# Moving the end of one attention and its router to another PSUM bank, with new orders for the queues

## The chip, the cores and the metric

The kernel runs on one core of one Trainium2 chip. The metric is the device time of one execution in microseconds. Before the change three runs gave 3598.25, 3603.09 and 3603.4 us, a median of 3603.09 us.

## The reference, cut to what matters

The input is 16 sequences of 512 rows with 128 channels. Two layers follow each other, and in each an attention and a feed-forward part work side by side on the same normalised input. In the first layer the feed-forward part is itself an attention (with its own layer norm, a convolution and rotary positions) followed by a mixture of experts.

```python
x = L0_attn_x                                   # 16 x 512 x 128
xn = layernorm(x)
x = x + L0_attn(xn, W_K, W_Q, W_V, W_O) \       # 16 heads of 64
      + L0_ffn(xn, ...)                         # _attn (16 heads of 8), then _moe
xn = layernorm(x)
x = x + L1_attn(xn, ...) + L1_ffn(xn, ...)      # flash blocks of 64; fp4 rounding

def _L0_ffn_ref(x, ...):
    x = x + _attn(x, ...)       # softmax(q k / sqrt(8)) v, then @ proj_w
    x = x + _moe(x, ...)        # layernorm, logits = h @ router_w, argmax of 4 experts
```

The change concerns the end of `_attn` (division by the softmax sum, the product with `proj_w`, the residual) and the start of `_moe` (layer norm, logits, argmax, and the rank of each row among the rows of its expert).

## The kernel before

The 16 sequences go through a software pipeline. `run(i, nxt, nn, prv)` is written for each engine and issues, interleaved, the work of four sequences: the wide attention and the experts of sequence `i` (called dense), the end of the narrow attention of `i` (after), the narrow attention of the next one (ahead), the first norm and projections of the one after that (early), and the second layer of the one before (behind). A loop turn of this kind is called a sequence here. Each engine works its own queue in order. The order is written out by hand in `ORDERS` (line 140), one list of named steps for each engine, and `walk` calls them. Semaphores, named after what is done, join the engines. SyncE has an order of its own: `keep_xn`, `project_v` (which loads `xres`), `load_sorted`, `load_x`, `shift_rows`, `split` 0 and 1 (nine loads each of the stacks `qst` and `kst`), `store_out`.

PSUM is one tensor `ps` of 8 banks of 512 columns. Banks 0 to 3 are a ring for the wide attention (`kq`, `scores`) and serve the experts later. Bank 4 takes `v`, `z`, `transpose1`, `project`, `attend`. Banks 5 and 6 take the narrow attention: `project_v` (5), `row_max` (5 and 6 in turn), `exps` (the same), and before them the end of the narrow attention of the sequence before: `divide` (5 and 6 in turn), `join` (5), `project_y` (6), `transpose3` (5), `route` (6), `rank` (5). Bank 7 takes the second layer, from `transpose2` to `down1`.

The steps that the text below speaks of:

- `divide(t)`: TensorE turns `ys` (line 1753), VectorE takes the reciprocal of the sums and multiplies (lines 1293, 1294). `join`: TensorE turns the result (through the helper at line 1538), ScalarE copies it (960). `project_y`: product (1763), VectorE adds the residual (1301). `begin`, `ln3_stats`, `ln3_root`, `ln3_apply`: VectorE. `transpose3`, `route` (1773): TensorE; VectorE's `route` finds the expert. `rank` (1781 to 1786); `place` on VectorE ends with the semaphore `placed` (1359), for which `scatter` on GpSimd and `project_v` on TensorE wait.
- `scores(p, t)`: TensorE (1584, 1587), then the row maximum on VectorE (1210), then the exponential on ScalarE (877). Each waits for the unit two before it in the ring. `norm(p)`: VectorE (1181) and GpSimd (722) make `vn`, on which `z(p)` (1601) waits. `kq` (1561) is copied by ScalarE (858).
- `transpose2` (1538), `keys1` (1796), `queries1` (1804), `values1` (1810), `scores1` (1819): start of the second layer of the sequence before; each is copied from bank 7 by ScalarE or VectorE before the next one may write it.
- `row_max(u)`: TensorE (1703, 1705), VectorE (1275), 44 units. `exps(u)` (1722, 1724): 44 units, ScalarE (945). `attend` (1743).
- `round_h(t, k)`: the fp4 rounding, k = 0 to 2 on VectorE, the last on GpSimd (lines 798 to 800). `transpose_hq(t)` (1877) waits for it, `down1` (1884) for all four, and VectorE adds the result (1464).
- `gather` on GpSimd (789, 792) waits until the expert results are stored; `take_over` on VectorE (1367) waits for what it fetches.

Of the kernel before, what the change touches and what calls it, by code (L numbers as in the profile page):

```python
# [7 lines left out]
ALU = mybir.AluOpType  # L8
ACT = mybir.ActivationFunctionType
# [8 lines left out]
NT = T // P  # L18
# [117 lines left out]
for _p in range(PAIRS):  # L136
# [25 lines left out]
        ("row_max", 39), ("scores", 7, 1), ("row_max", 40), ("row_max", 41), ("probs_T1", 1, 3), ("scores", 7,
        2), ("row_max", 42), ("z", 6), ("scores", 7, 3), ("row_max", 43), ("mix1", 1), ("project1",),
        ("shift_rows",), ("z", 7), ("sort",), ("exps", 0), ("exps", 1), ("ao",), ("gate", 0), ("exps", 2),
        ("value", 0), ("gate", 1), ("exps", 3), ("exps", 4), ("transpose1",), ("value", 1), ("turn", 0),
        ("attend", 0, 0), ("exps", 5), ("exps", 6), ("transpose_xq",), ("down", 0), ("gate", 2), ("value", 2),
        ("exps", 7), ("exps", 8), ("turn", 1), ("exps", 9), ("attend", 0, 1), ("exps", 10), ("attend", 0, 2),
        ("exps", 11), ("attend", 0, 3), ("gate1", 0), ("down", 1), ("exps", 12), ("exps", 13), ("up1", 0),
# [113 lines left out]
def build_layers(nc, w, x, consts, out, h_sorted, y_sorted):  # L282
    B = x.shape[0]
    with ExitStack() as ctx:
# [540 lines left out]
        def _(act):  # L825
# [21 lines left out]
            def run(i, nxt, nn, prv):  # L847
# [1079 lines left out]
```

## Time and profile before

| | |
|---|---|
| median of three runs | 3603.09 us |
| the profiled execution | 3598.52 us |
| its span, first to last instruction | 3596.7 us |
| mean granted TensorE clock | 0.937 |
| TensorE matmul busy | 3086.5 us, 86% |
| VectorE busy | 2093.3 us, 58% |
| ScalarE busy | 1787.1 us, 50% |
| GpSimd busy | 860.3 us, 24% |

Read it from the busiest engine: what counts is where TensorE stands idle and for whom it waits there. The list of waits gives the sum of each kind, the timeline the place. As the pipeline repeats, one sequence in the middle stands for the others, and the windows say whether it does. The granted clock is 1.00 at 2.4 GHz and 0.50 at 1.2 GHz.

### The profile page before, as it was taken

The page shows a single profiled execution, that of the slowest core. Times are in us where ns is not written, and L with a number is a line of the kernel's source. Part 1 is how long each engine was busy: PE and PEld are TensorE (multiplying, and loading weights), DVE is VectorE, ACT ScalarE, POOL GpSimd, SP SyncE. Part 2 cuts the span into 40 slices and gives each one's busy share as a digit, 9 for nine tenths or more (in the row PEclk, how much of TensorE's full clock was granted, in tenths as well). Part 3 has the DMA queues.
Part 4 walks back from the last instruction along what each step waited for, and adds up shares of the span by engine and source line. Part 5 has one row for each costly group of instructions (what it writes and reads, how often), then busy time and mean ns, then how long its engine had stood idle before and what let it go on. Part 6 is the DMA issues. An engine that isn't in the chain of part 4 may idle for free.

```text
span 3596.7 us, 53224 instructions
## 1 busy us (share of the span) xinstructions
PE 3086.5 (86%) x19535; PEld 1705.8 (47%) x19535; DVE 2093.3 (58%) x4810; ACT 1787.1 (50%) x4252; POOL 860.3 (24%) x1140
## 2 busy tenths in 40 slices
PE   2689898998989899998989889898988989898864
PEld 1245455454545545454545545454554545454432
DVE  5454665756566575657656565665656566554432
ACT  0245555555545455555545555554555555455421
POOL 0000222313222131323123132312213131222323
PEclk7699999999999999999999999999999999999965
DMA  4130303020020302002030301103020110200000
GB/s 104 20 44 1 52 2 47 9 36 20 13 43 2 55 2 44 12 17 40 1 55 2 44 12 22 35 2 55 2 44 12 24 31 7 47 2 14 6 11 3
DMA packets 112901, 89.39 MB, mean 25 GB/s; under 512 B 11203, under 2 KB 107269, under 8 KB 112645
## 3 DMA queue, kind: packets, MB, share of 16 engines
q1 hardware_dynamic: 93956, 70.25, 12.8%
q0 software_dynamic: 4096, 8.40, 0.8%
q10 hardware_dynamic: 14592, 7.34, 0.7%
q8 instruction: 159, 2.61, 0.3%
q14 instruction: 98, 0.79, 0.1%
HBM read 27.05 MB, written 16.19 MB: 12 GB/s over the span
## 4 chain that ended last, share of the span: by engine, by line
PE 59%; DVE 12%; POOL 10%; issue 9%; ACT 5%; DMA 2%; SPq 1%; POOLq 0%; ACTq 0%; DVEq 0%
PE ps L1584 6%; PE ps L1601 6%; PE ps L1819 4%; PE ps L1743 4%; PE ps L1722 4%; PE ps L1656 3%; PE ps L1645 3%; PE ps L1623 3%; DVE nma L1210 3%; PE ps L1632 3%; PE ps L1574 2%; PE ps L1703 2%; PE ps L1884 2%; PE ps L1561 2%; PE ps L1587 2%
## 5 line engine op out<-in xcount | busy, mean ns | idle before, releaser
L877 ACT ACTIVATE share_a<-ps,nma 128x128 f32<-128x128 f32 (+3 forms) x1024 | 530.9, 525 | 443.7 <-DVE nma L1210 442.5
L1210 DVE TENSOR_REDUCE nma<-ps 128x2 f32<-128x256 f32 (+3 forms) x512 | 420.1, 823 | 407.5 <-PE ps L1587 405.4
L945 ACT ACTIVATE share_z<-ps 128x512 f32<-128x512 f32 (+1 forms) x704 | 378.3, 559 | 372.1 <-PE ps L1724 241.7
L1275 DVE TENSOR_REDUCE nmx<-ps 128x1 f32<-128x384 f32 (+3 forms) x704 | 426.1, 635 | 173.9 <-PE ps L1705 162.4
L722 POOL TENSOR_TENSOR vn<-va,rla 128x512 f32<-128x512 f32 x128 | 133.4, 1042 | 1359.1 <-DVE rla L1181 1359.1
L1601 PE MATMUL ps<-share_a,vn 128*64 128x512 f32 (+3 forms) x2048 | 351.4, 492 | 35.7 <-POOL vn L722 34.7
L1703 PE MATMUL ps<-kst,qst 96*128 96x128 bf16 (+3 forms) x1024 | 269.6, 317 | 71.1 <-DMA kst<-part 34.4
L1722 PE MATMUL ps<-qst,kst 99*128 99x512 bf16 (+3 forms) x1024 | 261.6, 304 | 28.2 <-ACT share_z L945 14.9
L798 POOL TENSOR_TENSOR share_s<-share_s 128x352 f32<-128x352 f32 (+1 forms) x80 | 80.1, 1001 | 770.7 <-DVE share_s L1084 770.5
L1601 PEld LDWEIGHTS ps<-share_a,vn 128*64 128x64 f32 x2048 | 150.8, 151 | 227.9 <-issue 154.2
L1584 PE MATMUL ps<-kq_odd 64*128 64x128 f32 (+3 forms) x1024 | 220.5, 508 | 38.7 <-ACT share_a L877 36.9
L1561 PE MATMUL ps<-xnTd,wkqT 128*128 128x512 f32 x512 | 245.3, 601 | 1.6
L1584 PE MATMUL ps<-share_g 64*128 64x128 f32 (+3 forms) x1024 | 209.9, 486 | 39.5 <-ACT share_a L877 37.6
L1743 PE MATMUL ps<-share_z,vones 128*32 128x512 f32 (+3 forms) x2048 | 193.8, 451 | 15.2 <-ACT xnTd L921 12.3
L1705 PE MATMUL ps<-up_b,ident_b 128*128 128x128 bf16 x1024 | 205.6, 228 | 0.0
L877 ACT ACTIVATION_READ_ACCUMULATOR share_a<-ps,nma 128x1 f32 x1024 | 203.1, 198 | 0.0
L1722 PEld LDWEIGHTS ps<-qst,kst 99*128 99x128 bf16 x1024 | 99.4, 98 | 216.3 <-ACT share_z L945 110.9
L1724 PE MATMUL ps<-low_b,ident_b 128*128 128x128 bf16 x1024 | 195.9, 221 | 0.0
L1703 PEld LDWEIGHTS ps<-kst,qst 96*128 96x128 bf16 x1024 | 103.1, 101 | 174.7 <-DVE nmx L1275 102.7
L1819 PE MATMUL ps<-share_q,share_s 128*128 128x512 f32 x256 | 151.1, 673 | 32.4 <-ACT share_s L982 24.7
L1574 PE MATMUL ps<-wvT,xnTd 128*128 128x128 f32 x1024 | 147.4, 288 | 29.2 <-ACT share_z L882 28.8
L1587 PEld LDWEIGHTS ps<-up_b,ident_b 128*128 128x128 bf16 x1024 | 58.4, 97 | 236.8 <-issue 221.4
(250 smaller groups left out, 5727.0 us busy)
## 6 DMA issues: line engine op xcount, KB each, us to landing
qst<-part SPq DMA_DIRECT2D x144, 128.0 KB
kst<-part SPq DMA_DIRECT2D x144, 128.0 KB
share_r<-h_sorted SPq DMA_DIRECT2D x16, 448.0 KB, 3.5
y_sorted<-share_a ACTq DMA_DIRECT2D x16, 448.0 KB, 3.0
xin<-in_L_attn_x SPq DMA_DIRECT2D x16, 256.0 KB, 3.9
xk<-xn SPq DMA_DIRECT2D x16, 256.0 KB, 17.5
xres<-in_L_attn_x SPq DMA_DIRECT2D x16, 256.0 KB
out<-xn SPq DMA_DIRECT2D x16, 256.0 KB, 17.4
```

What stands on the lines that cost most here:

```text
L877: activation(pa[:, h % 4, OFF[t]:OFF[t] + P * (t + 1)], ps[:, b + k, 0:P * (t + 1)], ACT.Exp, bias=nma[:, h, t:t + 1], accum_out=la[:, h, ...
L945: activation(pt[:, n % 2, h % 4:h % 4 + k, 0:wd], src, ACT.Exp, scale=SCALE_B)\
L1210: v.tensor_reduce(nma[:, 2 * p:2 * p + 2, t], ps[:, b:b + 2, 0:P * (t + 1)], AX.X, ALU.max, negate=True).then_inc(amax, 1)
L1275: v.tensor_reduce(nmx[:, h:h + k, t], src, AX.X, ALU.max, negate=True).then_inc(bmax_ready, 1)
L1561: ins = mm(ps[:, b + z, :], wkqT[:, z, 2 * DA * p:2 * DA * (p + 1)], xnTd[:, :], start=True, stop=True)
L1574: ins = mm(ps[:, 4, tile(t)], xnTd[:, tile(t)], wvT[:, 2 * DA * p:2 * DA * (p + 1)], start=True, stop=True)
L1584: mm(ps[:, b + k, 0:P * (t + 1)], kq[p % 2][rows, 0, tile(t)], kq[p % 2][rows, 1, 0:P * (t + 1)], start=True, stop=False)
L1601: ins = mm(ps[DA * k:DA * k + DA, 4, 0:P * (t + 1)], vn[:, h % 4, t, :], pa[:, h % 4, OFF[t]:OFF[t] + P * (t + 1)], start=(t == NT - 1), s ...
L1703: mm(ps[:, b, o:o + wd], qst[0:SHIFT_ROW, h, tile(t)], kst[0:SHIFT_ROW, h, 0:wd], start=True, stop=False)
L1722: mm(ps[:, b, o:o + wd], kst[0:SHIFT_ROW + PARTS, h, tile(j)], qst[0:SHIFT_ROW + PARTS, h, j * P:T], start=True, stop=False)
L1743: ins = mm(ps[32 * k:32 * k + 32, 4, j * P:T], vones[:, c0:c0 + 32], pt[:, n % 2, k, 0:T - j * P], start=(j == 0), stop=(j == NT - 1))
L1819: mm(ps[:, 7, :], qbd[:, 2 * p:2 * p + 2, :].rearrange("c h q -> c (h q)"), k1T, start=True, stop=False)
```

## The change

The six steps of the end of the narrow attention go from banks 5 and 6 to bank 7. For this TensorE's `divide` 1 to 3 wait until VectorE has read the one before, and `divide` 0 waits for the last add of the second layer; `project_v` no longer waits for `placed`, and `transpose2` does. All five lists in `ORDERS` are new. What the text below speaks of: on TensorE the divides are spread further apart, `project_y` comes ahead of `kq` 2 and next to it, `project_v` comes right after `z` 0, `rank` after `scores` 2,0, `up1` 3 ahead of `attend` 2,3, `transpose_hq` 2 after `turn_x`, `transpose_hq` 3 after `exps` 40, and `down1` ahead of `attend` 3,2. On VectorE `take_over` comes after `scores` 0,2, `ln2_stats` after `ln3_apply`, `split` 1 after `project` 1,1. On GpSimd `scatter` comes after `norm` 2, and `gather` after the last `round_h`.

```diff
 pool=[
-        ("norm", 0), ("norm", 1), ("spread_queries1",), ("scatter",), ("norm", 2), ("shift1", 0), ("shift1",
+        ("norm", 0), ("norm", 1), ("spread_queries1",), ("norm", 2), ("scatter",), ("shift1", 0), ("shift1",
...
-        ("gather",), ("round_h", 3, 3),
+        ("round_h", 3, 3), ("gather",),
...
 pe, the first half:
-        ("kq", 0), ("divide", 0), ("v", 0), ("divide", 1), ("kq", 1), ("scores", 0, 0), ("divide", 2),
-        ("divide", 3), ("v", 1), ("scores", 0, 1), ("join",), ("scores", 0, 2), ("project_y",), ("scores", 0,
-        3), ("kq", 2), ("scores", 1, 0), ("scores", 1, 1), ("scores", 1, 2), ("z", 0), ("v", 2), ("scores", 1,
-        3), ("transpose3",), ("kq", 3), ("route",), ("scores", 2, 0), ("scores", 2, 1), ("scores", 2, 2),
-        ("z", 1), ("rank",), ("v", 3), ("scores", 2, 3), ("kq", 4), ("transpose2",), ("project_v",),
-        ("keys1",), ("scores", 3, 0), ("queries1",), ("row_max", 0), ("values1",), ("row_max", 1), ("row_max",
+        ("kq", 0), ("divide", 0), ("v", 0), ("divide", 1), ("kq", 1), ("divide", 2), ("scores", 0, 0), ("v",
+        1), ("scores", 0, 1), ("divide", 3), ("scores", 0, 2), ("join",), ("scores", 0, 3), ("project_y",),
+        ("kq", 2), ("scores", 1, 0), ("scores", 1, 1), ("scores", 1, 2), ("z", 0), ("project_v",),
+        ("transpose3",), ("v", 2), ("scores", 1, 3), ("route",), ("kq", 3), ("scores", 2, 0), ("rank",),
+        ("scores", 2, 1), ("scores", 2, 2), ("z", 1), ("v", 3), ("scores", 2, 3), ("kq", 4), ("transpose2",),
+        ("keys1",), ("row_max", 0), ("row_max", 1), ("queries1",), ("values1",), ("scores", 3, 0), ("row_max",
...
 pe, the end:
-        33), ("attend", 2, 3), ("down", 6), ("exps", 34), ("up1", 3), ("exps", 35), ("exps", 36), ("exps",
-        37), ("exps", 38), ("turn_x",), ("attend", 3, 0), ("exps", 39), ("exps", 40), ("exps", 41), ("attend",
-        3, 1), ("exps", 42), ("exps", 43), ("transpose_hq", 2), ("attend", 3, 2), ("transpose_hq", 3),
-        ("attend", 3, 3), ("down1",),
+        ("down", 5), ("turn", 6), ("up1", 3), ("attend", 2, 3), ("exps", 34), ("down", 6), ("exps", 35),
+        ("exps", 36), ("exps", 37), ("exps", 38), ("turn_x",), ("transpose_hq", 2), ("attend", 3, 0), ("exps",
+        39), ("exps", 40), ("transpose_hq", 3), ("exps", 41), ("attend", 3, 1), ("exps", 42), ("exps", 43),
+        ("down1",), ("attend", 3, 2), ("attend", 3, 3),
...
@@ project_v (TensorE)
                         pe.wait_ge(xnTd_ready, count(i, DENSE["xnTd_ready"], 1))
-                        pe.wait_ge(placed, count(i, AHEAD["placed"], 1))
@@ divide (TensorE)
                     if t == 0:
                         pe.wait_ge(by_ready, count(i, AHEAD["by_ready"], 4))
-                    if t >= 2:
-                        pe.wait_ge(yn_ready, count(i, AHEAD["yn_ready"], t - 1))
+                        if prv is not None and (type(prv[0]) is not int or prv[0] + prv[1]):
+                            pe.wait_ge(out_ready, count(prv, BEHIND["out_ready"], 0))
+                    else:
+                        pe.wait_ge(yn_ready, count(i, AHEAD["yn_ready"], t))
                     for g in range(4):
-                        ins = tr(ps[:, 5 + t % 2, tile(g)], ys[:, g, tile(t)], idn)
+                        ins = tr(ps[:, 7, tile(g)], ys[:, g, tile(t)], idn)
@@ transpose2 (TensorE)
                     pe.wait_ge(xn2_ready, count(prv, BEHIND["xn2_ready"], 4))
+                    if i is not None:
+                        pe.wait_ge(placed, count(i, AHEAD["placed"], 1))
                     transpose_tiles(xn2, 7).then_inc(xn2T_psum, 1)
```

## Rows read from the trace of the kernel before

**Rows 1.** The page: the span, and busy time of the engines.
```profile
span 3596.7 us, 53224 instructions
PE 3086.5 (86%) x19535; PEld 1705.8 (47%) x19535; DVE 2093.3 (58%) x4810; ACT 1787.1 (50%) x4252; POOL 860.3 (24%) x1140
```
**Rows 2.** Windows between two `down1` adds: us, busy by engine, PEclk, DMA share, GB/s.
```profile
1199.22:1407.33 208.11, 188.75 (x1219) 105.53 (x1218) 129.00 (x298) 111.03 (x265) 53.77 (x71) 0.97 0.15 25
...
1615.45:1820.55 205.10, 183.51 (x1219) 103.64 (x1218) 129.14 (x299) 111.13 (x265) 53.81 (x71) 0.99 0.16 25
...
2445.31:2653.35 208.04, 187.11 (x1219) 104.82 (x1218) 128.99 (x298) 111.24 (x265) 53.78 (x71) 0.98 0.16 25
```
**Rows 3.** List of waits, whole span: us in total, times, longest us.
```profile
PE ps L1877 <- POOL share_q L800: 50.5, 18, 9.2
```
**Rows 4.** Timeline of TensorE, end of a sequence: start us, us, instruction [idle before].
```profile
1186.20 1.06 PE L1743 MATMUL ps<-share_z,vones 128*32 128x512 f32 x8 [0.77 <-ACT xnTd L921]
...
1193.66 0.55 PE L1877 MATMUL ps<-ident,share_q 128*128 128x128 f32 x3 [2.37 <-POOL share_q L800]
...
1194.78 4.33 PE L1884 MATMUL ps<-wdT,share_s 128*128 128x128 f32 x24
```
**Rows 5.** Timeline of GpSimd in the same stretch.
```profile
1185.43 0.37 POOL L789 TENSOR_TENSOR turn_g<-vones 1x1 f32<-1x1 f32 x1 [4.22 <-DMA y_sorted<-share_a]
1185.96 1.06 POOL L792 DMA_INDIRECT yg<-y_sorted,place_i  x1 [0.15 <-issue]
...
1189.83 0.94 POOL L792 DMA_INDIRECT yg<-y_sorted,place_i  x1 [0.30 <-issue]
1190.80 0.95 POOL L798 TENSOR_TENSOR share_s<-share_s 128x352 f32<-128x352 f32 x1
```
**Rows 6.** Timeline of VectorE in the same stretch, the last operation of `round_h` 3,2.
```profile
1186.17 0.34 DVE L1084 TENSOR_SCALAR share_s<-share_s 128x352 f32<-128x352 f32 x1
```
**Rows 7.** Timeline of TensorE, the first 42 us of the next sequence.
```profile
1200.67 0.60 PE L1753 MATMUL ps<-ident,share_r 128*128 128x128 f32 x4
...
1205.36 1.15 PE L1753 MATMUL ps<-ident,share_r 128*128 128x128 f32 x8 [0.40 <-DVE share_r L1294]
...
1214.91 0.49 PE L1584 MATMUL ps<-kq_odd 64*128 64x128 f32 x4 [0.86 <-ACT share_a L877]
...
1221.78 1.16 PE L1574 MATMUL ps<-wvT,xnTd 128*128 128x128 f32 x8 [0.69 <-ACT share_z L882]
...
1230.36 0.92 PE L1584 MATMUL ps<-share_g 64*128 64x384 f32 x4 [1.52 <-ACT share_a L877]
...
1231.43 4.06 PE L1601 MATMUL ps<-share_a,vn 128*64 128x512 f32 x16
...
1236.18 1.16 PE L1574 MATMUL ps<-wvT,xnTd 128*128 128x128 f32 x8 [0.40 <-ACT share_z L882]
...
1240.96 0.66 PE L1538 MATMUL ps<-ident,xn 128*128 128x128 f32 x4 [0.57 <-DVE xn L1064]
```
**Rows 8.** Timeline of VectorE, `divide` 0 of that sequence.
```profile
1204.72 0.26 DVE L1293 RECIPROCAL rb<-ps 128x16 f32<-128x16 f32 x1
1205.01 0.29 DVE L1294 TENSOR_TENSOR share_r<-ps,rb 128x128 f32<-128x128 f32 x1
```
**Rows 9.** Timeline of TensorE, `z` 1 two sequences later.
```profile
1647.67 2.37 PE L1601 MATMUL ps<-share_a,vn 128*64 128x512 f32 x16
```
**Rows 10.** Timeline of ScalarE, the copy of `transpose2`.
```profile
1241.65 0.59 ACT L970 COPY share_s<-ps 128x512 f32<-128x512 f32 x1 [0.29 <-PE ps L1538]
```
**Rows 11.** Timeline of SyncE's queue: the issue of the `kst` loads.
```profile
1200.27 13.93 SPq L671 DMA_DIRECT2D kst<-part  x9
```
**Rows 12.** Window in which the loads end (columns as in rows 2).
```profile
1230.00:1235.00 5.00, 4.64 (x20) 1.89 (x22) 2.79 (x14) 2.46 (x10) 1.04 (x1) 0.69 0.23 72
1235.00:1240.00 5.00, 4.60 (x32) 2.47 (x28) 3.08 (x12) 1.26 (x3) 0.00 (x0) 0.97 0.00 0
```
**Rows 13.** Timeline of TensorE, last but one sequence, `transpose_hq` 3.
```profile
3455.89 0.90 PE L1877 MATMUL ps<-ident,share_q 128*128 128x128 f32 x3 [9.23 <-POOL share_q L800]
```

More of the change, by code:

```diff
@@ L162 @@
[L162 to L166, printed above, removed]
@@ new lines @@
+        41), ("row_max", 42), ("z", 6), ("scores", 7, 3), ("row_max", 43), ("mix1", 1), ("project1",),
+        ("shift_rows",), ("z", 7), ("sort",), ("exps", 0), ("exps", 1), ("ao",), ("gate", 0), ("value", 0),
+        ("exps", 2), ("exps", 3), ("transpose1",), ("transpose_xq",), ("gate", 1), ("value", 1), ("turn", 0),
+        ("exps", 4), ("attend", 0, 0), ("exps", 5), ("exps", 6), ("gate1", 0), ("down", 0), ("gate", 2),
+        ("exps", 7), ("exps", 8), ("value", 2), ("turn", 1), ("exps", 9), ("attend", 0, 1), ("exps", 10),
@@ new lines @@
+        ("attend", 0, 2), ("exps", 11), ("attend", 0, 3), ("exps", 12), ("up1", 0), ("down", 1), ("exps", 13),
+        ("project", 0, 0), ("gate", 3), ("exps", 14), ("exps", 15), ("project", 0, 1), ("value", 3), ("turn",
+        2), ("gate1", 1), ("exps", 16), ("attend", 1, 0), ("exps", 17), ("exps", 18), ("down", 2), ("exps",
+        19), ("attend", 1, 1), ("exps", 20), ("exps", 21), ("gate", 4), ("attend", 1, 2), ("exps", 22),
+        ("exps", 23), ("attend", 1, 3), ("value", 4), ("turn", 3), ("exps", 24), ("up1", 1), ("project", 1,
@@ new lines @@
+        0), ("down", 3), ("gate", 5), ("transpose_hq", 0), ("value", 5), ("turn", 4), ("exps", 25),
+        ("project", 1, 1), ("exps", 26), ("gate1", 2), ("down", 4), ("attend", 2, 0), ("exps", 27), ("exps",
+        28), ("up1", 2), ("gate", 6), ("exps", 29), ("exps", 30), ("value", 6), ("transpose_hq", 1), ("turn",
+        5), ("exps", 31), ("attend", 2, 1), ("exps", 32), ("attend", 2, 2), ("exps", 33), ("gate1", 3),
+        ("down", 5), ("turn", 6), ("up1", 3), ("attend", 2, 3), ("exps", 34), ("down", 6), ("exps", 35),
@@ L190 @@
[L190 to L193 removed]
+        ("divide", 0), ("divide", 1), ("divide", 2), ("scores", 0, 0), ("scores", 0, 1), ("divide", 3),
@@ new lines @@
+        ("scores", 0, 2), ("take_over",), ("scores", 0, 3), ("project_y",), ("begin",), ("ln3_stats",),
+        ("scores", 1, 0), ("scores", 1, 1), ("norm", 0), ("ln3_root",), ("scores", 1, 2), ("ln3_apply",),
+        ("ln2_stats",), ("scores", 1, 3), ("route",), ("scores", 2, 0), ("scores", 2, 1), ("norm", 1),
+        ("scores", 2, 2), ("place",), ("ln2_root",), ("scores", 2, 3), ("ln2_apply",), ("row_max", 0),
+        ("row_max", 1), ("values1",), ("row_max", 2), ("row_max", 3), ("row_max", 4), ("row_max", 5),
@@ L207 @@
[L207 to L208 removed]
+        43), ("mix1", 1), ("norm", 7), ("project1",), ("shift_rows",), ("ln0_stats",), ("ln0_root",),
+        ("round_x", 0), ("round_x", 1), ("round_x", 2), ("ln0_apply",), ("ln1_apply",), ("add_ao",), ("gate",
+        0), ("value", 0), ("gate", 1), ("value", 1), ("gate", 2), ("conv",), ("up1", 0), ("project", 0, 0),
@@ L232 @@
-        ("exps", 32), ("down", 5), ("turn", 6), ("gate1", 3), ("exps", 33), ("attend", 2, 3), ("down", 6),
-        ("store_y",), ("exps", 34), ("exps", 35), ("exps", 36), ("exps", 37), ("exps", 38), ("turn_x",),
-        ("exps", 39), ("exps", 40), ("exps", 41), ("exps", 42), ("exps", 43), ("transpose_hq", 2),
-        ("transpose_hq", 3), ("attend", 3, 3),
[4 rows of a table added]
+        ("kq", 5), ("scores", 4, 0), ("scores", 4, 1), ("scores", 4, 2), ("z", 3), ("v", 5), ("scores", 4, 3),
[4 rows of a table added]
+        1, 3), ("scores", 7, 2), ("z", 6), ("scores", 7, 3), ("z", 7), ("sort",), ("exps", 0), ("exps", 1),
@@ new lines @@
+        ("exps", 22), ("exps", 23), ("attend", 1, 3), ("turn", 3), ("down", 3), ("gate", 5), ("exps", 24),
+        ("transpose_hq", 0), ("turn", 4), ("exps", 25), ("exps", 26), ("gate1", 2), ("exps", 27), ("exps",
+        28), ("down", 4), ("gate", 6), ("exps", 29), ("transpose_hq", 1), ("exps", 30), ("exps", 31), ("turn",
+        5), ("exps", 32), ("exps", 33), ("gate1", 3), ("down", 5), ("turn", 6), ("attend", 2, 3), ("exps",
+        34), ("down", 6), ("store_y",), ("exps", 35), ("exps", 36), ("exps", 37), ("exps", 38), ("turn_x",),
```

110 lines of the change are left out of this document (44 added, 66 removed), and 15 rows, old and new, of the table act.

## The prediction

> **What bounds the kernel now.** I read the page first: TensorE is busy for 86% of a span of 3596.7 us and no other engine for more than 58% [rows 1], so the order in which TensorE's queue is worked off sets the time, and only an idle gap on TensorE, or a stretch in which it runs slowly, can be won. The profiled execution took 3598.52 us, 4.6 us less than the median of the runs (3603.09); the sum below is made against 3598.5. Next I cut the span at the last step of a sequence, the residual add of `down1`, and took the busy times between two of them [rows 2]. Between 574 and 3274 us there are 13 intervals of this kind. Eleven take 208.0 to 208.4 us, of which TensorE is busy 188.8 in most; one took 205.1 and the last one 204.1, as its loop turn has less to do. So there are some 19 us of gaps in a sequence, and 3 us more that come and go with the granted clock (0.97 against 0.99).
>
> Where the gaps lie I took from the list of waits and from the timeline of one sequence. The longest single one is the wait of the last `transpose_hq` for GpSimd [rows 3, 4]: 2.37 us in the sequence shown, and 2.35 to 2.55 us in each of the fourteen such steps. In the first 50 us of a sequence there are smaller ones, of which the change touches six [rows 7], by name: 0.40 (`divide` 2), 0.86 (`scores` 1,0), 0.69 (`v` 2), 1.52 (`scores` 2,2), 0.40 (`v` 3), 0.57 (`transpose2`). The second half of a sequence, from `sort` to `turn_x`, has hardly any: TensorE is the bound there, and the reshuffled steps of that part cannot bring much. I take them at nothing, with 0.5 us a sequence to either side.
>
> **The clock.** `z` 1 is the same work in each sequence. It takes 4.06 us in the one shown and 2.37 us in another [rows 7, 9]: the first ran at the lower of the two levels (1.2 GHz) and the second at 2.4 GHz, and what went before the slow one was the gap of 1.52 us. There are four slow stretches of this kind in a usual sequence, each behind a group of gaps; one of them is in the `down1` right behind the gap of 2.37 us. In the sequence of 205.1 us three of the four were missing, in that of 208.0 us only the last one [rows 2]: the last one is worth 0.1 us and the other two (208.1 - 205.1 - 0.1) / 2, about 1.4 us each. I use 1.4; the row of `z` 1 alone gives 1.7, the last stretch 0.1, and these are the ends.
>
> **The change, part by part.**
>
> *GpSimd's order at the end of a sequence.* The diff puts the last `round_h` ahead of `gather`. Before, VectorE had finished its share of that step at 1186.5 [rows 6], but GpSimd was in `gather`, which started at 1185.4 when the expert results had been stored, and issued four indirect transfers until 1190.8; only then came the three operations of `round_h` [rows 5], till `transpose_hq` could start at 1193.66 [rows 4]. Without `gather` in front they start at 1186.5 and end some 2.8 us later, at 1189.3. `up1` 3 also moves forward past `attend` 2,3, `exps` 34 and `down` 6, so VectorE is ready still earlier. The new place of `transpose_hq` 3, behind `exps` 40, is at about 1189.2. So the whole 2.37 us goes, and what comes next is TensorE's own work. `transpose_hq` 2 moves in between `turn_x` and `attend` 3,0, where TensorE waited 0.77 us for the copy [rows 4]; three transposes take a good 0.3 us there: gain 0.3. `gather` now runs from about 1189.3 to 1194.5. Its reader, `take_over`, moves on VectorE from ahead of the divides to behind `scores` 0,2, some 10 us later, so nobody waits. Sum 2.7 us in 14 sequences: 38 us. Beside it the slow stretch of `down1`: with the gap gone, I expect it to go too, 1.4 x 14 = 20 us (bounds 0 and 24).
>
> *One bank instead of two.* Nine steps (four `divide`, `join`, `project_y`, `transpose3`, `route`, `rank`) now write bank 7, and each `divide` waits for VectorE to have read the one before. A handover on VectorE takes 0.26 + 0.29 us and the hand-off on both sides [rows 8], so 0.75 us from the end of the transposes. Between two divides the new order has `v` 0, `kq` 1, and `scores` 0,0 with `v` 1 and `scores` 0,1, each at least 0.9 us. They hide it, if VectorE is free. Before, it wasn't: it began the first divide at 1204.72 [rows 8], 3.4 us after the transposes of `divide` 0 had ended [rows 7], for it still had `split` 1, `take_over` and the statistics to do. The diff moves all three away from there, so the wait of 0.40 us goes, and about 0.25 us come back at `join`. The Trainium skill ("PSUM — Partial Sum Buffer", section "PSUM bank collisions raise a hardware error") has it that TensorE and a reader may not be on one bank and quadrant at once and that one has to guard by bank. It speaks against this part: by it none of the nine handovers can be overlapped within itself, which is the slow rival below. The trace shows no violation and no price of one.
>
> *What now lies in the gaps.* `project_y` stands ahead of `kq` 2, so `scores` 1,0 is covered: 0.86 gained, and 0.25 lost as `scores` 1,1 then waits for the copy of `kq` 2. `project_v` (0.9 us) and `transpose3` fill the 0.69 us ahead of `v` 2: 0.45 gained, because VectorE's `ln3_root` is now ahead of `scores` 1,2 and delays ScalarE. `route` waits about 0.5 for two operations of ScalarE that now follow each other (0.59 each by [rows 10]). `rank` goes in behind `scores` 2,0, and VectorE's `route` ends before that; so the 1.52 us ahead of `scores` 2,2 go, but then `z` 1 waits about 0.9 for its normalised values: 0.5 gained. `v` 3 loses the cover of `rank`: 0.3 lost.
>
> *The start of the row maxima.* The wait for `placed` moves from `project_v` to `transpose2`. But every `row_max` still stands behind `transpose2` in TensorE's queue, so it still waits for the placement in effect. What is new is that `project_v` (0.9 us) no longer lies between `transpose2` and `keys1` and covers the copy of 0.59 us [rows 7, 10]: `keys1` waits 0.7. `values1` waits 0.45, since only the copy of the queries lies ahead of it. Both are lost. Together with the last paragraph: 0.15 + 0.86 - 0.25 + 0.45 - 0.5 + 0.5 - 0.3 - 0.7 - 0.45 = -0.2 us. A walk through the same steps in order, with start-to-start times, comes out 1 us better. I take 0, with 1 us to either side (15 us in all).
>
> *Transfers.* The 18 loads of the stacks are issued one by one from 1190.8 on; those of the keys took until 1214.2 and moved data until about 1233 [rows 11, 12]. The first `row_max` came after `transpose2`, which started at 1240.96 [rows 7]. It moves forward by some 5 us at most against the loads: still hidden. *The tail.* The last but one sequence has a gap of 9.23 us at the same place [rows 13], but little else hangs on it: `gather` gives back all but some 3 us.
>
> Sum: 38 + 20 + 0 + 3 = 61 us; 3598.5 - 61 = 3537. **Forecast 3537 us.**
>
> **The rivals.**
> *(a) The clock gives more.* If the slow stretch of `z` 1 goes too, another 14 x 1.4 = 20 us: 3517. For it: the gap of 1.52 ahead of it is split up. Against it: by the sum above 0.5 and 0.9 us stand there instead.
> *(b) The clock takes.* If a slow stretch comes up behind `transpose2`, where 0.6, 0.7 and 0.45 us now lie close together, or that of `down1` stays: 3557; both: 3577. The Trainium skill ("TensorE: Matmul & The Clock Gate", section "A second HAM failure mode: psum-queue depth-cycling") tells of a kernel whose small idles between groups of matmuls while cycling through PSUM banks made the clock go up and down. By that rule the change tends to this rival; the trace agrees so far as `z` 1 ran at the lower level behind a gap of 1.52 us [rows 7].
> *(c) Slower: the single bank shows.* If VectorE is late at the divides as it was before, the handovers lie open. Nine of 0.75 us are 6.8 us, with a slow stretch 8.2, against the 4.1 us gained at the end: (8.2 - 4.1) x 15 = 62 us slower, 3660. It turns to slower from the point where more than five of the nine are uncovered. Against it: what kept VectorE is moved away.
> *(d) No change.* What is won at the end is waited for again at the stacks' loads, or at `take_over`: 3598. It needs the loads to end 10 us later than they do.
> *(e) The change doesn't do what it says*: the maxima don't start sooner against the placement. I hold this to be true, and it costs nothing, as the gain is from elsewhere; if the new order at the end didn't act either, it would be (d).
>
> **How the numbers follow.** Forecast 0.52, (a) 0.16, (b) 0.16, (c) 0.08, (d) 0.08. The likeliest case by itself runs from 3515 to 3560 (15 us of the first half, 7 of the second, the bounds of the clock). For 8 in 10 the range takes in (a) and (b): 3495 to 3585. A measurement can tell about 0.2%, 7 us. Faster by more: 0.86; within: 0.05; slower by more: 0.09.
>
> **What would show it.** On GpSimd `round_h` stands ahead of the indirect transfers, and the wait of `transpose_hq` for GpSimd falls from 2.4 us to nearly nothing. `down1` takes less than 4.3 us. TensorE's waits at `scores` 1,0 and `v` 2 shrink, and new ones of 0.5 to 0.7 stand at `keys1` and `values1`. Each `divide` waits under 0.3 us. The sequence falls from 208.1 to about 204. Wrong would be: a gap at the divides, a granted clock below 0.97, or a wait of the first `row_max` for the stacks.

## The result, and the profile after

The changed kernel takes 3570.06 us in the median, the kernel before 3602.35; the ratio is 0.991, with a 95% interval of 0.989 to 0.993. So it is faster, by 32 us. The forecast was 3537 us, a gain of 61 us against the profiled execution or 66 against the median: about half of it did not come. The profiled execution took 3563.68 us.

The page after, its span and the busy times, beside [rows 1]:

```profile
span 3561.9 us, 53255 instructions
...
PE 3055.1 (86%) x19535; PEld 1694.9 (48%) x19535; DVE 2179.6 (61%) x4810; ACT 1777.2 (50%) x4252; POOL 858.2 (24%) x1140
```

TensorE has lost 31 us of busy time with the same instructions. VectorE has 86 us more of it with the same 4810 instructions. Nobody added work to VectorE, and that is the first thing that the forecast doesn't explain.

Windows from one `down1` add to the next, of the kernel after, columns as in [rows 2]; the last line adds up ten of them (775.84 to 2834.70):

```profile
1188.91:1394.49 205.58, 186.54 (x1219) 104.87 (x1219) 134.69 (x299) 110.41 (x265) 53.61 (x71) 0.98 0.15 25
...
1602.47:1806.07 203.60, 184.52 (x1219) 103.48 (x1217) 134.62 (x299) 110.43 (x265) 53.61 (x71) 0.98 0.15 25
...
sum 2058.86, PE 1859.95 PEld 1044.86 DVE 1347.49 ACT 1104.39 POOL 536.14; mean PE 186.00 PEld 104.49 DVE 134.75 ACT 110.44 POOL 53.61
```

The same line for the kernel before, ten sequences (782.82 to 2861.56):

```profile
sum 2078.74, PE 1880.83 PEld 1051.42 DVE 1289.99 ACT 1111.04 POOL 537.36; mean PE 188.08 PEld 105.14 DVE 129.00 ACT 111.10 POOL 53.74
```

A sequence went from 207.9 to 205.9 us. TensorE's busy time fell from 188.1 to 186.0 us, the same work at a better clock. Its idle time is (2078.74 - 1880.83) / 10 = 19.8 us before and (2058.86 - 1859.95) / 10 = 19.9 us after: as long as it was, although the wait of 2.37 us at the end is gone. VectorE is busy for 5.7 us more in each sequence.

The timeline of TensorE, after, one sequence (its `down1` add stands at 1188.91):

```profile
1185.21 2.89 PE L1887 MATMUL ps<-wdT,share_s 128*128 128x128 f32 x24
...
1206.26 0.92 PE L1584 MATMUL ps<-kq_odd 64*128 64x384 f32 x4 [1.17 <-ACT share_a L877]
...
1221.07 2.37 PE L1601 MATMUL ps<-share_a,vn 128*64 128x512 f32 x16 [0.83 <-POOL vn L722]
...
1224.13 1.16 PE L1574 MATMUL ps<-wvT,xnTd 128*128 128x128 f32 x8 [0.69 <-ACT share_z L882]
...
1230.31 1.13 PE L1799 MATMUL ps<-share_s,w1T 128*128 128x512 f32 x2 [0.68 <-ACT share_s L970]
...
1233.05 1.16 PE L1813 MATMUL ps<-w1T,share_s 128*128 128x128 f32 x8 [0.40 <-ACT q1T L978]
...
1267.21 0.39 PE L1702 MATMUL ps<-kst,qst 96*128 96x512 bf16 x1 [3.83 <-DVE nmx L1275]
```

`down1` (L1887) takes 2.89 us where it took 4.33 [rows 4], and `z` 1 takes 2.37 instead of 4.06 [rows 7]. The last row is new: a `row_max` that waits 3.83 us for VectorE, in nine of the fourteen full sequences 5.48 us. The lists of waits show the same, first after, then before (us in total, times, longest):

```profile
PE ps L1702 <- DVE nmx L1275: 77.5, 42, 5.5
```

```profile
PE ps L1703 <- DVE nmx L1275: 34.2, 67, 0.9
```

What VectorE did ahead of it is in its timeline, after, with GpSimd's below:

```profile
1254.59 1.60 DVE L1275 TENSOR_REDUCE nmx<-ps 128x1 f32<-128x384 f32 x3 [0.16 <-PE ps L1704]
1256.11 4.95 DVE L1396 TENSOR_TENSOR dm<-rm 128x56 f32<-128x56 f32 x1
```

```profile
1252.50 0.98 POOL L781 DMA_INDIRECT h_sorted<-xh,place_i  x1 [0.30 <-issue]
1253.50 7.47 POOL L739 TENSOR_TENSOR share_s<-share_s,rm 128x1024 f32<-128x1024 f32 x4
```

The same two instructions before, VectorE first:

```profile
1266.41 0.67 DVE L1396 TENSOR_TENSOR dm<-rm 128x56 f32<-128x56 f32 x1
```

```profile
1265.11 7.48 POOL L739 TENSOR_TENSOR share_s<-share_s,rm 128x1024 f32<-128x1024 f32 x4 [4.82 <-DVE rm L1386]
```

L1396 is the small subtraction of `shift1` 3: 56 columns, two operands in SBUF. It takes 0.67 us before and 4.95 us after, and ends at 1261.06, 0.1 us after GpSimd's four large subtractions (L739, `shift1` 0 to 3). Before, GpSimd stood idle for 4.82 us until the running maxima (L1386) were ready; after, the four follow `scatter` without a break, half a microsecond behind the maxima. `scatter` stood ahead of `norm 2` and now stands behind it. The diff shows that move, and the prediction doesn't price it.

L1396 accounts for 4.3 of the 5.7 us by which VectorE is busier in each sequence. The rest comes from one more meeting with GpSimd, in `ln0_apply` (L1064), which the new order brings beside the rounding of `round_x`. VectorE, then GpSimd, after:

```profile
913.82 4.03 DVE L1064 TENSOR_SCALAR xn<-xin,mv,ry 128x128 f32<-128x128 f32 x4
```

```profile
913.99 1.30 POOL L798 TENSOR_TENSOR share_s<-share_s 128x512 f32<-128x512 f32 x1 [9.21 <-DVE share_s L1084]
915.37 1.27 POOL L799 TENSOR_TENSOR share_s<-share_s 128x512 f32<-128x512 f32 x1
916.71 1.06 POOL L800 TENSOR_TENSOR share_s<-share_s,qm 128x512 f32<-128x512 f32 x1
```

The four of L1064 take 1.11 us in the kernel before; in exchange small steps of the norm (L1036 and L1039 above all), which met GpSimd there before, are 1.5 us shorter. The same 4.03 us stand in the fastest kernel below, so they are not the missing half.

### The profile page after: what moved, and what is told of

Read it like the earlier page. It is cut to its first block, busy times and chain, and to the rows that moved or that the text cites. A ratio compares the mean times of both kernels' runs of the same rounds, so it can differ in the third digit from the quotient of the medians.

```text
span 3561.9 us, 53255 instructions
## 1 busy us (share of the span) xinstructions
PE 3055.1 (86%) x19535; PEld 1694.9 (48%) x19535; DVE 2179.6 (61%) x4810; ACT 1777.2 (50%) x4252; POOL 858.2 (24%) x1140
## 3 DMA queue, kind: packets, MB, share of 16 engines
q8 instruction: 159, 2.61, 0.3%
## 4 chain that ended last, share of the span: by engine, by line
PE 67%; DVE 16%; ACT 6%; POOL 4%; issue 3%; DMA 2%; SPq 2%; ACTq 0%; POOLq 0%; DVEq 0%
PE ps L1584 8%; PE ps L1601 7%; PE ps L1742 5%; PE ps L1721 4%; PE ps L1822 4%; DVE nma L1210 4%; PE ps L1561 3%; PE ps L1656 3%; PE ps L1574 3%; PE ps L1645 3%; PE ps L1632 3%; PE ps L1623 3%; PE ps L1702 3%; PE ps L1587 2%; DVE dm L1396 2%
## 5 line engine op out<-in xcount | busy, mean ns | idle before, releaser
L1601 PE MATMUL ps<-share_a,vn 128*64 128x512 f32 (+3 forms) x2048 | 318.2, 454 | 23.5 <-POOL vn L722 22.4
L1584 PE MATMUL ps<-share_g 64*128 64x128 f32 (+3 forms) x1024 | 229.1, 527 | 10.0 <-ACT share_a L877 4.7
L1601 PEld LDWEIGHTS ps<-share_a,vn 128*64 128x64 f32 x2048 | 140.1, 141 | 199.6 <-issue 132.0
```

What stands on the lines that cost most here:

```text
L1584: mm(ps[:, b + k, 0:P * (t + 1)], kq[p % 2][rows, 0, tile(t)], kq[p % 2][rows, 1, 0:P * (t + 1)], start=True, stop=False)
L1601: ins = mm(ps[DA * k:DA * k + DA, 4, 0:P * (t + 1)], vn[:, h % 4, t, :], pa[:, h % 4, OFF[t]:OFF[t] + P * (t + 1)], start=(t == NT - 1), s ...
```

## Experiments

My theory after the comparison: VectorE's small subtraction and GpSimd's large ones get in each other's way, and the place of one against the other costs the missing half. The rival: it is `scatter`'s new place. Under test as well were the terms of the forecast. The kernel before took 3597.87 us (median) in the first group of runs (e1 to e4), 3603.35 in the second (i to l) and 3601.78 in the third (m to p).

**e1_shift_early.** The kernel after, with VectorE's order at this place put back.

```diff
-        ("row_max", 13), ("row_max", 14), ("row_max", 15), ("row_max", 16), ("shift1", 3), ("sum1", 0)
+        ("row_max", 13), ("shift1", 3), ("row_max", 14), ("row_max", 15), ("row_max", 16), ("sum1", 0)
```

> The changed kernel with one thing undone on VectorE: the small subtraction of shift1 3 stands ahead of row_max 14 again, as in the kernel before, instead of behind row_max 16. Theory: this operation (128x56, two operands in SBUF) took 4.95 us in the changed kernel, 0.67 us before, because it came up beside the later of GpSimd's four 128x1024 subtractions and ended only with the last of them; it held up VectorE's queue, and TensorE stood for 3.8 to 5.5 us at a row_max and ran slowly for one or two stretches behind it. So: the operation at most 1.9 us, the gap under 1 us, the sequence 3.5 to 5 us shorter, a time of 3505 to 3525 us against some 3570 for the changed kernel. Rival 1, the delay comes from scatter, which now stands ahead of shift1 on GpSimd: the time stays within 8 us of 3570. Rival 2, VectorE is just short of time there for its reductions: the gap of 4 to 5 us appears at another row_max and the time stays.

Measured: 3597.9 us, ratio 1.000 (0.999 to 1.001). The expectation missed: the whole gain of the change went. VectorE and TensorE:

```profile
1474.48 6.71 DVE L1396 TENSOR_TENSOR dm<-rm 128x56 f32<-128x56 f32 x1
```

```profile
1481.71 0.50 PE L1702 MATMUL ps<-kst,qst 96*128 96x384 bf16 x1 [6.70 <-DVE nmx L1275]
```

The four large ones run from 1473.64 to 1481.11. The small one came in 0.84 us behind their start instead of 2.6 and ended with them again, so it took longer. VectorE's order had not been the mistake.

**e2_shift_late.** The kernel before, with that step of VectorE in the place that it has after.

```diff
-        ("shift1", 3), ("row_max", 14), ("row_max", 15), ("row_max", 16), ("sum1", 0)
+        ("row_max", 14), ("row_max", 15), ("row_max", 16), ("shift1", 3), ("sum1", 0)
```

> The kernel before with this one thing alone: the subtraction of shift1 3 moved behind row_max 16 on VectorE, as in the changed kernel. Theory: it takes 4 to 6 us instead of 0.67, a gap of 3 to 5 us stands at a row_max, and the time rises by 14 x 2.5 to 5 us, to 3635 to 3670 us. Rival 1 (scatter) and rival 2 (VectorE short of time) expect no change, within 7 us of 3602.

Measured: 3597.32 us, ratio 1.000 (0.999 to 1.001); the small subtraction takes 1.02 us:

```profile
1678.30 1.02 DVE L1396 TENSOR_TENSOR dm<-rm 128x56 f32<-128x56 f32 x1
```

Another miss, and the other half of the answer: with `scatter` in its early place the small one is let in at the end of the one of the four that it meets, the first before and the second here.

**e4_scatter_back.** The kernel after, with `scatter` alone put back.

```diff
-        ("norm", 0), ("norm", 1), ("spread_queries1",), ("norm", 2), ("scatter",), ("shift1", 0)
+        ("norm", 0), ("norm", 1), ("spread_queries1",), ("scatter",), ("norm", 2), ("shift1", 0)
```

> The changed kernel with scatter on GpSimd put back ahead of norm 2. Theory (the slow subtraction is at fault): GpSimd's four subtractions start only 0.5 us sooner, as scatter had ended 0.5 us after the maxima were ready, the small operation stays at 4 to 5 us, and the time stays within 8 us of the changed kernel's 3570. Rival 1 (scatter is at fault): the gap at the row_max falls by over 2 us and the time to 3535 us or less.

Measured: 3510.2 us, ratio 0.976 (0.975 to 0.978). The theory as it stood (the slow subtraction alone, whatever `scatter` does) missed, and its rival held. That is 88 us faster than before in the same group, and faster than the change by 60 us between the medians (53 by the two ratios, since the kernel before differs by some 4 us between the groups). VectorE, GpSimd, TensorE, and the sum over ten sequences (765.87 to 2789.86):

```profile
1439.24 0.76 DVE L1396 TENSOR_TENSOR dm<-rm 128x56 f32<-128x56 f32 x1
```

```profile
1436.17 7.48 POOL L739 TENSOR_TENSOR share_s<-share_s,rm 128x1024 f32<-128x1024 f32 x4 [4.73 <-DVE rm L1386]
```

```profile
1446.51 0.39 PE L1702 MATMUL ps<-kst,qst 96*128 96x512 bf16 x1 [2.10 <-DVE nmx L1275]
```

```profile
sum 2023.99, PE 1858.75 PEld 1046.93 DVE 1305.49 ACT 1100.24 POOL 535.53; mean PE 185.87 PEld 104.69 DVE 130.55 ACT 110.02 POOL 53.55
```

The four start 1.86 us apart (7.48 less the last one's 1.90, by three). The small one came at 1439.24, 3.07 us behind the first start, and ended at 1440.00, just behind the end of the second (1436.17 + 2 x 1.86 = 1439.89). In the kernel after it came 2.61 us behind the start and was passed over at the ends of the second and the third. A sequence takes 202.4 us, idle time 16.5.

**j_scatter_late.** The kernel before, with `scatter` alone moved as the change moves it.

```diff
-        ("spread_queries1",), ("scatter",), ("norm", 2), ("shift1", 0)
+        ("spread_queries1",), ("norm", 2), ("scatter",), ("shift1", 0)
```

> The kernel before with one step of GpSimd moved: scatter goes behind norm 2, directly ahead of shift1 0, as in the kernel after; nothing else is changed. My theory expects the small subtraction L1396 on VectorE to take 4.5 to 6.7 us instead of 0.67, a gap of 3 us or more at a row_max behind it, and 3640 to 3670 us (3598 and 14 or 15 sequences of 3 to 4.8 us). The rival (scatter's place costs time only together with the earlier row maxima of the kernel after) expects L1396 under 1.5 us or no gap behind it, and 3590 to 3605 us.

Measured: 3688.57 us, ratio 1.024 (1.022 to 1.026): the small subtraction did what was expected, and the time was worse than its range. GpSimd, then VectorE:

```profile
1727.06 0.96 POOL L781 DMA_INDIRECT h_sorted<-xh,place_i  x1 [0.31 <-issue]
1728.04 7.47 POOL L739 TENSOR_TENSOR share_s<-share_s,rm 128x1024 f32<-128x1024 f32 x4
```

```profile
1729.00 6.60 DVE L1396 TENSOR_TENSOR dm<-rm 128x56 f32<-128x56 f32 x1
```

One step moved on an engine that is busy for a quarter of the span costs 85 us. The idle time of TensorE is 25.5 us a sequence, from the windows as above, the busy time 188.2 as before. The change's new place of `shift1` 3, behind three row maxima, softens it: 53 to 60 us instead of 85. With that step moved back (e1 against e4) it is 88 again.

**i_shift_past.** The kernel after, `scatter` late, and VectorE's small subtraction moved past GpSimd's four.

```diff
-        ("shift1", 3), ("sum1", 0), ("sum1", 1), ("scores", 3, 3), ("sum1", 2)
+        ("sum1", 0), ("sum1", 1), ("scores", 3, 3), ("shift1", 3), ("sum1", 2)
```

> The kernel after with one step of VectorE moved: shift1 3, whose first instruction is the small subtraction dm<-rm (L1396), stands behind sum1 1, ahead of sum1 2. Scatter keeps its new late place. My theory (VectorE's small subtraction, which reads two operands of SBUF, is kept out as long as GpSimd works through its four large subtractions without a break) expects it to start after GpSimd's fourth one has ended, to take 0.2 to 0.3 us instead of 4.95, the gap of TensorE ahead of row_max to fall under 2.0 us, and 3505 to 3525 us. Rival A (the late scatter delays the chain at this place by itself: the maxima, the exponentials or the loads behind it come later) expects the gap of 3.8 to 5.5 us to stay and 3560 to 3575 us, as in the kernel after. Rival B (the consumers of dm, blend1 and mix1, now come too late) expects a new wait at mix1 0 and over 3575 us.

Measured: 3511.9 us, ratio 0.975 (0.973 to 0.976). GpSimd, then VectorE:

```profile
1642.82 7.47 POOL L739 TENSOR_TENSOR share_s<-share_s,rm 128x1024 f32<-128x1024 f32 x4
```

```profile
1651.44 0.21 DVE L1396 TENSOR_TENSOR dm<-rm 128x56 f32<-128x56 f32 x1
```

With `scatter` still late the whole loss is gone. So its price is that of the small subtraction; what the same move of VectorE's step is worth with `scatter` early was not run. The row shown is one of six in which it came behind the four and took 0.2 us. In nine others it came 0.3 us ahead of the end of the last one, took 0.40 us and ended with it. The gap at `row_max` fell to 2.1 us in most sequences, not under 2.0: ahead of that maximum VectorE now has its sums to do.

**l_e4_backlog, m_e4_backlog36, o_tiny_between.** What decides whether the small subtraction is let in after one or two of the four, or only after all? Either the indirect transfers directly ahead or that GpSimd comes late to work that is ready. In l and m `scatter` is early, and tiny multiplications keep GpSimd busy ahead of the four, 30 or 36 of them; in o `scatter` is late and three tiny ones stand behind it.

```diff
 def shift1(k):
+    if k == 0:
+        ...
+        for n in range(30):
+            nc.gpsimd.tensor_tensor(idle[:, n:n + 1], vones[0:1, VCOLS - 1:VCOLS],
+                                    vones[0:1, VCOLS - 1:VCOLS], ALU.mult).then_inc(idle_turn, 1)
     pool.wait_ge(rm_ready, count(prv, BEHIND["rm_ready"], 1))
```

> The fastest kernel so far (the kernel after with scatter back ahead of norm 2) with 30 tiny multiplications of one element on GpSimd ahead of its first large subtraction (shift1 0): GpSimd then comes to the four subtractions late and with all of them ready, but no indirect DMA stands directly ahead. It tells which of two things holds VectorE's small subtraction (L1396) up over more than one of them. If it is that GpSimd has fallen behind and issues the four back to back, L1396 takes 4 us or more, the gap at row_max is 3 us or more, and the time is 3550 us or more. If it takes the indirect transfers directly ahead, L1396 stays under 1.9 us, which is the length of one of the four, the gap at row_max stays near 2.1 us and the time is 3505 to 3530 us.

> The fastest kernel with scatter in its early place, and 36 tiny multiplications of one element on GpSimd ahead of shift1 0 instead of 30. In l_e4_backlog GpSimd was done with the 30 and waited for 0.34 us for the running maxima, so it had not fallen behind; with 36 it comes some 0.5 us after them, as behind the late scatter of the kernel after. If falling behind is what makes VectorE's small subtraction wait for all four large ones, it takes 4 us or more (4.95 in the kernel after), and the time is 3545 us or more. If the indirect transfers ahead are what makes it, it takes under 1 us and the time is 3503 to 3525 us.

> The kernel after, scatter late, with three tiny multiplications of one element between scatter and shift1 0: GpSimd's four large subtractions start some 0.5 us later than in the kernel after, and what stands directly ahead of them is no indirect transfer. If it takes the indirect transfer directly ahead, the small subtraction of VectorE falls to under 1.9 us and the time to 3510 to 3530 us. If indirect transfers shortly ahead, or the backlog, do it, it takes 4.9 to 5.6 us and the time is 3565 to 3585 us.

Measured: 3508.03, 3572.82 and 3558.15 us, one run each. In these three kernels the lines are 7 further down: L746 and L1403 are the large and the small subtraction. GpSimd and VectorE in l:

```profile
1231.90 4.46 POOL L741 TENSOR_TENSOR idle<-vones 1x1 f32<-1x1 f32 x30
1236.71 7.48 POOL L746 TENSOR_TENSOR share_s<-share_s,rm 128x1024 f32<-128x1024 f32 x4 [0.34 <-DVE rm L1393]
```

```profile
1239.74 0.80 DVE L1403 TENSOR_TENSOR dm<-rm 128x56 f32<-128x56 f32 x1
```

In m:

```profile
1462.69 5.37 POOL L741 TENSOR_TENSOR idle<-vones 1x1 f32<-1x1 f32 x36
1468.02 7.47 POOL L746 TENSOR_TENSOR share_s<-share_s,rm 128x1024 f32<-128x1024 f32 x4
```

```profile
1470.53 5.04 DVE L1403 TENSOR_TENSOR dm<-rm 128x56 f32<-128x56 f32 x1
```

In o:

```profile
1459.25 0.47 POOL L741 TENSOR_TENSOR idle<-vones 1x1 f32<-1x1 f32 x3
1459.68 7.47 POOL L746 TENSOR_TENSOR share_s<-share_s,rm 128x1024 f32<-128x1024 f32 x4
```

```profile
1461.86 5.38 DVE L1403 TENSOR_TENSOR dm<-rm 128x56 f32<-128x56 f32 x1
```

Six tiny instructions more, and the small subtraction takes 5.04 us instead of 0.80, in each of the fourteen full sequences, and the kernel 65 us longer. Run l was meant to hold GpSimd up and did not: GpSimd was done with the 30 and still waited for 0.34 us, so l only shows that busy time on GpSimd ahead is harmless. In m it came 0.6 us behind the maxima, with no indirect transfer near; in o the transfers stand near but not directly ahead, and it came 1.0 us behind the maxima. (The time of o, 3558 us, lies between its two ranges; the 5.38 us are as expected for being late.) Being late decides, the indirect transfers don't. Nor does the point at which the small one arrives: in e2 it came 0.95 us into one of the four and was let in at its end, in j 0.96 us into one and was not.

**e3_pool_only.** Now the terms of the forecast. The kernel before, with the last `round_h` ahead of `gather` on GpSimd and nothing else.

```diff
-        ("gather",), ("round_h", 3, 3),
+        ("round_h", 3, 3), ("gather",),
```

> The kernel before with one swap on GpSimd: the last round_h ahead of gather, nothing else. Theory of the prediction: the wait of transpose_hq 3 for GpSimd falls from 2.4 us to nearly nothing, since its new end (1189.3 in the trace of before) lies ahead of TensorE's arrival at 1191.3, and the slow stretch of down1 goes with it: 14 x (2.4 + 1.4) = 53 us less, 3549 us. Rival: the clock gives nothing back here, 14 x 2.4 = 34 us less, 3568 us. Rival: take_over, which stands early on VectorE in this order, now waits for the later gather, and all is given back: 3600 us.

Measured: 3669.29 us, ratio 1.019 (1.017 to 1.021), slower. VectorE, then TensorE:

```profile
1646.96 0.69 DVE L1367 TENSOR_TENSOR xp<-xacc,yg 128x512 f32<-128x512 f32 x1 [8.09 <-DMA yg<-y_sorted,place_i]
```

```profile
1650.25 1.97 PE L1753 MATMUL ps<-ident,share_r 128*128 128x128 f32 x8 [8.58 <-DVE share_r L1294]
```

The wait of `transpose_hq` for GpSimd is gone, but the last gather, issued at 1634.13, lands at 1646.96, beside the stack loads. `take_over` heads VectorE's queue and waits for it, and behind it wait the divides.

**p_end_alone.** The same, with `take_over` and `ln2_stats` moved on VectorE too.

```diff
-        ("take_over",), ("ln2_stats",), ("divide", 0), ... ("scores", 0, 2), ("project_y",), ... ("scores", 1, 3)
+        ("divide", 0), ... ("scores", 0, 2), ("take_over",), ("project_y",), ... ("ln2_stats",), ("scores", 1, 3)
```

> The kernel before with the end of the sequence changed alone: on GpSimd round_h 3,3 stands ahead of gather, and on VectorE take_over moves behind scores 0,2 and ln2_stats ahead of scores 1,3, as in the kernel after. TensorE's order, its banks and scatter's place are those of before. The step of the prediction under test: this edit is worth 2.37 us of waiting and 1.4 us of slow clock in down1 for each of 14 sequences, so 3598 - (33 to 53) = 3545 to 3565 us, with no gap of more than 0.5 us at the divides. The rival (the gain of 88 us comes mainly from the first half of the sequence: banks, divides, project_v, rank) expects 3575 to 3600 us here. Over 3620 us would show that gather's transfers, which came late in e3_pool_only, are still waited for.

Measured: 3562.08 us, ratio 0.988 (0.987 to 0.990), a gain of 40 us, within its range. TensorE at the end of a sequence (the window cuts the row after 20 of its 24 instructions), and the sum over ten (786.08 to 2837.68):

```profile
2015.77 2.50 PE L1884 MATMUL ps<-wdT,share_s 128*128 128x128 f32 x20 [0.88 <-ACT share_s L1009]
```

```profile
sum 2051.60, PE 1864.45 PEld 1044.07 DVE 1291.07 ACT 1109.07 POOL 534.93; mean PE 186.44 PEld 104.41 DVE 129.11 ACT 110.91 POOL 53.49
```

Idle time falls by 1.1 us a sequence, not by 2.4: with TensorE's order of before, `down1` waits 0.4 to 1.0 us for ScalarE's copy of the last transposes instead, in ten of fourteen sequences. Busy time falls by 1.6. The profiled execution is the slowest of the four (3573.52 us), so these rows rather understate the gain.

**k_e4_gather_back.** The fastest kernel with this one step of GpSimd undone.

```diff
-        ("round_h", 3, 3), ("gather",),
+        ("gather",), ("round_h", 3, 3),
```

> The fastest kernel so far (the kernel after with scatter back ahead of norm 2, 3510.2 us) with one more step of GpSimd put back: gather stands ahead of round_h 3,3 again. The step of the prediction under test: GpSimd's order at the end of a sequence is worth 38 us of waiting and 20 us of slow clock in down1. The step as predicted expects the wait of transpose_hq 3 for GpSimd to be back at 1.5 to 2.5 us in each sequence and 3544 to 3568 us. The rival (transpose_hq 3 now stands further ahead of the end and attend 3,2 and 3,3 behind it, so that the wait has less or more weight; or most of the gain of 88 us came from elsewhere) expects under 3530 us if the gain is from elsewhere, or over 3580 us if the wait has grown since transpose_hq 3 stands earlier.

Measured: 3648.36 us, ratio 1.014 (1.012 to 1.015), 138 us over its base between the medians and 134 by the ratios. TensorE:

```profile
2050.28 0.90 PE L1880 MATMUL ps<-ident,share_q 128*128 128x128 f32 x3 [6.25 <-POOL share_q L800]
```

The rival held: `transpose_hq` 3 stands some 4 us further forward in TensorE's new order, so it waits 6.25 us instead of 2.37, and the granted clock pays on top (busy time 188.0 us a sequence instead of 185.9).

**n_e4_max_first.** An attempt at the 2.1 us that are left at `row_max`.

```diff
-        ("sum1", 2), ("sum1", 3), ("row_max", 17), ("row_max", 18)
+        ("row_max", 17), ("sum1", 2), ("row_max", 18), ("sum1", 3)
```

> The fastest kernel (after with scatter back ahead of norm 2) with two steps of VectorE's order moved: row_max 17 goes ahead of sum1 2, and row_max 18 ahead of sum1 3. The wait of 2.11 us at a row_max, the longest one left in that part of the sequence, has VectorE's sums ahead of it. If it is VectorE's order that holds the maxima up, the wait falls by 1.0 to 2.0 us and the time to 3480 to 3500 us; if the wait only moves to the next scores or z, the time stays at 3503 to 3515 us; if the totals on GpSimd and mix1 come late by it, over 3515 us.

Measured: 3539.8 us, ratio 0.982 (0.980 to 0.984), slower than its base by 30 us between the medians, 20 by the ratios. VectorE, then TensorE:

```profile
1883.62 0.55 DVE L1408 RECIPROCAL bm<-ll 128x64 f32<-128x64 f32 x1 [2.51 <-POOL ll L748]
```

```profile
1884.63 3.70 PE L1601 MATMUL ps<-share_a,vn 128*64 128x512 f32 x14 [1.86 <-POOL vn L722]
```

The wait at this `row_max` fell to 0.4 us, but GpSimd's totals now start later, and `ratios1` stands on VectorE and waits 2.51 us for them, with the scores behind it. The waits came up again at `scores` and `z`.

## Why the prediction was half right

*The end of the sequence: right.* `round_h` goes first, the wait for GpSimd is gone, `down1` runs at 2.4 GHz. The gaps of the last 18 us of a sequence, taken from TensorE's timeline over ten sequences, come to 4.1 us a sequence before and 1.4 in e4, so the 2.7 that were forecast came. That `take_over` has to move for it was named, and e3 shows its price: 71 us lost instead of 40 won.

*The slow stretch of `down1`, 1.4 us: right, but not the whole.* `down1` went from 4.33 to 2.89 us, 1.44 less. Beside it `z` 1 went from 4.06 to 2.37, as rival (a) had it. Of these 3.1 us the better clock leaves 2.1 a sequence in the kernel after and 2.2 in e4 (188.1 us busy against 186.0 and 185.9), since other stretches at 1.2 GHz come up, some of them behind the gap at `row_max`.

*The first half, 0 with 1 us to either side: the single terms were mostly right.* Forecast at `z` 1 0.9 us, at `keys1` 0.7, at `values1` 0.45, at `v` 3 0.7; measured 0.83, 0.68, 0.40, 0.69. The waits at the divides are gone, so rival (c) did not come. Three small terms were off: `scores` 1,2 waits 1.17 us (0.47 before), for which the sum has nothing; `scores` 1,0 still waits 0.29; and the waits put down at `join` and `route` did not come. Together the gaps of the first 50 us fell from 6.3 to 5.7 us a sequence, within the range given. What all else in the change brings shows in p against e4: (2051.60 - 2023.99) / 10 = 2.8 us a sequence, and 88 - 40 = 48 us in all, more than half. Some 1.1 us of it are gaps in the last 18 us of a sequence (2.5 against 1.4), 0.7 gaps in its first 50. Which of the many moves bring the 48 us, I did not take apart.

*The step that failed: the sum lacks the move of `scatter`.* It is one entry on GpSimd's list, ahead of `norm 2` before and behind it after. The change's description names the move, but the prediction priced only the end of GpSimd's list: `scatter` stands in none of its terms and in no rival, so it was put at nothing without a reason. It looked at the first 50 us of a sequence, at the part from `sort` on and at the end; the stretch from 50 to 90 us, where this move acts, has no term in it. TensorE stands idle there for 6.5 us a sequence before, 9.1 after and 6.2 in e4. Ten sequences of e4 take 34.9 us less than those of the kernel after, nearly all of it idle time (16.5 against 19.9 us a sequence), and the runs differ by 53 to 60 us. Without this move the kernel gains 88 us where the forecast had 61; with it 32. So two errors of opposite sign stand in the sum: some 27 us too little for what was seen, and 53 to 60 us for what was not. The measured 3570.06 us lies inside the stated range of 3495 to 3585, but as the remainder of these two, which is luck: what `scatter` costs is none of the cases that the range was made from.

*What could have been seen before.* The row of GpSimd's L739 in the trace of before says that it waited for VectorE's running maxima after 4.82 us of idle time. `scatter`'s four transfers take some 5 us [rows 5 shows four of the same kind from 1185.96 to 1190.77]. Moved into 4.82 us of slack they turn a wait into a delay. The delay alone, about 0.5 us, would have looked like nothing; its price is that VectorE is kept out for the whole chain, and only the duration of L1396, 0.67 us for 56 columns where others of its size take 0.2, gives a hint of that in the trace of before.

*Rival (e)* holds as written: the maxima do not start sooner against the placement, 6.6 us behind its end before and 8.1 after in the two sequences shown.

## What to carry to other kernels

Price every entry that moves on every queue, and first those of the engine with the lowest busy share: ask whether it still waits for the next work or comes late to it. A small instruction of VectorE with two operands in SBUF, beside a run of large GpSimd instructions that GpSimd comes late to, cost up to 88 us here: put it behind the run, or keep GpSimd early. Either one brought the time back to 3510 to 3512 us. Terms of an order are not additive: one step of GpSimd won 40 us together with its partner on VectorE, lost 71 without it, and is worth over 130 in the final order.

## What the runs showed of the hardware

VectorE's subtraction of 128x56 took 0.2 us alone. It took 0.67 to 1.02 us when it met GpSimd's four 128x1024 subtractions and GpSimd had waited ahead of the first of them, and 4.95 to 6.71 us when GpSimd had come late to them (in the last but one sequence, which is shorter, 1.27 and up to 7.80). In each late case (after, e1, j, m, o) it ended within 0.1 us of the end of the fourth, having passed the ends of at least two. VectorE's reductions, which read one operand, ran beside the same four undisturbed (1.60 us for three maxima in the kernel after, 1.59 before).

The four instructions of `ln0_apply` (L1064) were held up too, though each reads one operand of 128x128 (and two columns): 4.03 us beside the three of `round_x`, 1.11 us in the kernel before. There GpSimd stood idle for 9.21 us ahead of the first of its three and for 0.08 us ahead of each of the others, and one instruction of VectorE was let in at the end of each.

The Trainium skill ("SBUF — State Buffer", sections "Who interferes with whom" and "SBUF: two separate sides") says that an instruction of VectorE with two SBUF inputs contends with a GpSimd instruction that reads SBUF, and that whoever issues first has the port for the whole instruction. The trace agrees that the subtraction is blocked, and the runs in which GpSimd had waited fit the rule, with 0.67 to 1.02 us. But by that rule the wait would always end with one instruction of 1.90 us, and in the late cases it lasted for three or four; the measurement decides. Why a GpSimd that comes late keeps the port from one instruction to the next, and one that waited lets it go, no run here shows.

The best version of this study is e4_scatter_back at 3510.2 us; i_shift_past, with 3511.9 us in another group of runs (ratios 0.976 and 0.975), can't be told from it.
